# Two-layer transformer block on one core: the heads' way to the output projection, through TensorE's transposes or through DRAM

## What is computed

```python
# B, T, C, H, D = 8, 512, 256, 16, 16
def attend(q, k, v, mask=None):             # heads of 16 columns, scale 1/4
    att = einsum('bhqd,bhkd->bhqk', q, k) * scale
    if mask is not None: att = where(mask, att, -inf)
    return einsum('bhqk,bhkd->bhqd', softmax(att, axis=-1), v)
# layer 0: causal self-attention and cross-attention share the queries' tokens; the two results are added
n = layernorm(x)
y = attend(n @ Wq + bq, n @ Wk + bk, n @ Wv + bv, causal) \
  + attend(n @ Wcq + bcq, ctx @ Wck + bck, ctx @ Wcv + bcv)
x = x + merge_heads(y) @ Wp + bp
x = x + bitlinear(gelu(bitlinear(layernorm(x), w1, b1)), w2, b2)   # int8 per token, ternary weights
# layer 1: cross-attention, then an FFN with one int8 scale for the whole tensor
n = layernorm(x)
x = x + merge_heads(attend(n @ Wq + bq, ctx @ Wk + bk, ctx @ Wv + bv)) @ Wo + bo
x = x + qlinear(gelu(qlinear(layernorm(x), w1, b1)), w2, b2)
```

## Time and profile before

| | |
|---|---|
| median of three runs | 2200.6 us (2190.96 to 2205.16) |
| span of the profiled execution | 2195.8 us |
| TensorE busy | 1773.6 us, 81% |
| VectorE busy | 1367.3 us, 62% |
| ScalarE busy | 1184.4 us, 54% |
| GpSimd busy | 727.3 us, 33% |
| DMA, mean share of 16 engines | 26% on the kernel's own queue |

### The profile page before, as it was taken

One profiled execution on the slowest core, in us unless ns is written; L12 is line 12 of the kernel. 1 busy time (PEld: TensorE's weight loads), 2 busy tenths in 40 slices (PEclk: granted clock), 3 DMA queues, 4 the chain that ended last, 5 costly groups with the idle time before them and its releaser, 6 DMA issues.

```text
span 2195.8 us, 35331 instructions
## 1 busy us (share of the span) xinstructions
PE 1773.6 (81%) x10144; PEld 758.5 (35%) x10144; DVE 1367.3 (62%) x2522; ACT 1184.4 (54%) x2245; POOL 727.3 (33%) x981
## 2 busy tenths in 40 slices
PE   2748488998789879997989788988898788768487
PEld 1214233442344324422443244323442343222124
DVE  2545566667656575667566766676566657354587
ACT  1135247555755566555755484547555754716484
POOL 4214052543244325431553135331543242230012
PEclk8679698999899989998999899998999899869699
DMA  3332331333132312332132213231333121030303
GB/s 105 87 89 59 87 102 30 90 88 104 30 83 74 94 49 73 98 87 56 45 100 77 77 45 97 75 98 31 85 82 95 36 83 35 1 106 1 134 10 124
DMA packets 107134, 160.46 MB, mean 73 GB/s; under 512 B 20673, under 2 KB 83265, under 8 KB 106945
## 3 DMA queue, kind: packets, MB, share of 16 engines
q1 hardware_dynamic: 102048, 156.96, 25.7%
q10 hardware_dynamic: 4896, 1.18, 0.3%
HBM read 105.52 MB, written 51.38 MB: 71 GB/s over the span
## 4 chain that ended last, share of the span: by engine, by line
PE 44%; POOL 14%; DVE 13%; issue 11%; ACT 8%; DMA 6%; SPq 3%; ACTq 0%; DVEq 0%; POOLq 0%
PE acc L1263 10%; PE mx L1228 10%; PE st L1249 8%; DVE nmax L1040 6%; PE misc L1203 4%; PE misc L1175 3%; POOL qk L725 3%; PE misc L1215 3%; POOL parts L727 3%; POOL parts L723 3%; PE misc L1290 2%; POOL parts L729 2%; PE misc L1317 1%; PE misc L1304 1%; DMA hid<-in_L_ffn_w_dram 1%
## 5 line engine op out<-in xcount | busy, mean ns | idle before, releaser
L1040 DVE TENSOR_REDUCE nmax<-mx 128x1 f32<-128x512 f32 (+2 forms) x1376 | 877.8, 673 | 504.6 <-PE mx L1228 313.8
L820 ACT ACTIVATE probs<-st 128x512 f32<-128x512 f32 (+3 forms) x1536 | 771.6, 549 | 592.8 <-PE st L1249 386.2
L1228 PE MATMUL mx<-stack 96*128 96x512 bf16 (+3 forms) x1536 | 570.5, 383 | 205.1 <-DVE nmax L1040 136.5
L1249 PE MATMUL st<-stack 99*128 99x512 bf16 (+3 forms) x1536 | 565.8, 377 | 68.5 <-ACT probs L820 51.0
L1228 PEld LDWEIGHTS mx<-stack 96*128 96x128 bf16 x1536 | 154.2, 101 | 429.6 <-DVE nmax L1040 308.1
L1249 PEld LDWEIGHTS st<-stack 99*128 99x128 bf16 x1536 | 151.5, 100 | 418.6 <-ACT probs L820 249.2
L723 POOL TENSOR_TENSOR parts<-qk,zero 128x512 bf16<-128x512 f32 x96 | 99.7, 1039 | 321.8 <-ACT qk L803 321.8
L735 POOL TENSOR_TENSOR nparts<-nmax,zero 128x16 bf16<-128x16 f32 x96 | 20.5, 214 | 403.8 <-DVE nmax L1040 396.5
L1263 PE MATMUL acc<-probs,v_x 128*32 128x512 f32 x1024 | 153.0, 673 | 0.0
L1263 PE MATMUL acc<-probs,v_f 128*32 128x512 f32 x1024 | 142.5, 630 | 0.4 <-ACT probs L820 0.3
L725 POOL TENSOR_TENSOR qk<-qk,parts 128x512 f32<-128x512 f32 x96 | 111.0, 1156 | 7.5
(11 more groups left out here) (213 smaller groups left out, 2164.1 us busy)
## 6 DMA issues: line engine op xcount, KB each, us to landing
parts_xk<-parts SPq DMA_DIRECT2D x48, 128.0 KB
parts_xq<-parts SPq DMA_DIRECT2D x48, 128.0 KB
stack<-parts_xq SPq DMA_DIRECT2D x32, 192.0 KB, 3.2
stack<-parts_xk SPq DMA_DIRECT2D x32, 192.0 KB, 3.6
parts_sk<-parts SPq DMA_DIRECT2D x48, 128.0 KB
parts_sq<-parts SPq DMA_DIRECT2D x48, 128.0 KB
stack<-parts_sq SPq DMA_DIRECT2D x32, 192.0 KB, 2.8
stack<-parts_sk SPq DMA_DIRECT2D x32, 192.0 KB, 3.3
```

What stands on the lines that cost most here:

```text
L820: act.activation(probs[:, j % P_SLOTS, c, T - w:], st_bank(n, 4 * j + c)[:, 0:w], ACT.Exp, scale=SCALE).then_inc(exp_done, 1)
L1040: dve.tensor_reduce(nmax[:, ring, first:first + NT * (len(cs) - 1) + 1:NT], src, AX.X, ALU.max, negate=True).then_inc(mx_free, 1)
L1228: last = pe.matmul(o, stack[0:ROWS, r, 0, c, P * i:P * i + P], stack[0:ROWS, r, 1, c, 0:w], start=True, stop=not causal)
L1249: last = pe.matmul(o[:, 0:w], stack[0:AUG, r, 1, c, P * j:P * j + P], stack[0:AUG, r, 0, c, T - w:T], start=True, stop=not causal)
```

## The change

The divided heads no longer go through TensorE. They go through DRAM:

- `heads_copy` writes one of two buffers. `heads_send` (SyncE, place 4 of the next slot) stores it, 128 x 512 fp32, 256 KB, to DRAM.
- For each pair of units (g = 1 and g = 3) `pair_fetch` (SyncE, place 7) reads the pair's denominators back densely as 128 x 32 (16 KB), and the 16 rows of each of the eight heads into yT, 128 x 512 (256 KB): the layout that the output projection reads.
- `pair_recip` (VectorE, place 11) takes one reciprocal of 128 x 32; `rec_send` (SyncE, place 12) stores it, 16 KB; `rec_bcast` (SyncE, place 15) reads it back with each head's row repeated on its 16 partitions, 128 x 512.
- `pair_mult` (GpSimd, place 3 of the slot after that) multiplies yT by it. `y_sum` (GpSimd) adds the two attentions in the same layout. In the last turn the last pair of layer 0 takes shorter distances (FAST), and `close` does all of it in a row.
- `heads_out` and `y_T` are gone. There are three yT now, one for each attention.
- Steps move. `ctx_T`, v and the key projections of f (`context1`) move from slots 3 and 4 to slot 0, from place 4 on. `layer1_end` begins in slot 1 at place 4 rather than slot 0 at place 6; layer 0's FFN and the rest of layer 1's start follow it. `layer0_end` moves from slot 8 to slots 9 and 10, with the projections of s behind it in slots 10 and 11. In the last turn `layer0_end` moves from slot 8 to slot 9, and the v of layer 1's last batch stays in AFTER.
- Statistics of the FFN's norm wait for the residual's second read in every batch (before, only in the last). Smaller: the tail's bias row is scaled in place.

```diff
+PLACES = {"heads_send": 4, "pair_fetch": 7, "pair_recip": 11, "rec_send": 12, "rec_bcast": 15}
+FAST = {"heads_send": 3, "pair_fetch": 6, "pair_recip": 8, "rec_send": 8, "rec_bcast": 10, "pair_mult": 13}
...
-            if (j, c) == (1, 1) and prev:
-                out.append(("heads_out", prev))
+            if (j, c) == (0, 3) and pair(back) and not after_fast:
+                out.append(("pair_mult", back))
+            if prev:
+                out += [(name, prev) for name, k in at.items() if k == HU * j + c and (pair(prev) or name == "heads_send")]
...
-    return [("values", u, NT - 1), ("heads_copy", u), ("heads_out", u)]
+    return [("values", u, NT - 1), ("heads_copy", u), ("heads_send", u), ("pair_fetch", u), ("pair_recip", u),
+            ("rec_send", u), ("rec_bcast", u), ("pair_mult", u)]
...
+def project_q(b, p):
+    return [x for m in range(KC) for x in (("project", b, p + "q", m), None, None, None)] + [("settle", b, p)]
...
-    return [("mid_bias", b), ("y_T", b, "A"), None, None, ("residual", b, "A"), None]
+    return [("mid_bias", b), ("y_sum", b), None, None, ("residual", b, "A"), None]
...
-    return [("stats", b, "C"), None, ("ctx_T", b, "C"), None, None, ("norm", b, "C"), None, ("norm_T", b, "C"), None]
+    return [("stats", b, "C"), None, None, None, ("norm", b, "C"), None, ("norm_T", b, "C"), None]
...
+def context1(b):
+    return [("ctx_T", b, "C"), None, ("v", b, "f"), None] + [x for m in range(KC) for x in (("project", b, "fk", m), None, None)]
 
...
-    return layer1_norm(b) + project(b, "f")
+    return layer1_norm(b) + project_q(b, "f")
...
-    return [("y_T", b, "C"), None, ("residual", b, "C"), None, ("stats", b, "E"), None, None, ("norm", b, "E"),
+    return [("residual", b, "C"), None, ("stats", b, "E"), None, None, ("norm", b, "E"),
...
-        start = slots(us[:5], [None] * 6 + layer1_end(b - 2) + layer0_ffn(b - 1) + layer1_start(b - 1), b + more)
+        start = slots(us[:1], [None] * 4 + context1(b - 1), b + more) + \
+            slots(us[1:5], [None] * 6 + layer1_end(b - 2) + layer0_ffn(b - 1) + layer1_start(b - 1), b + more)
...
-            slots(us[8:9], [None] * 6 + layer0_end(b), b) + \
-            slots(us[9:12], layer0_ffn(b) + [("load1", b)] + layer1_norm(b) + project_qk(b, "f"), b)
+            slots(us[8:9], [], b, fast=True) + \
+            slots(us[9:12], layer0_end(b) + layer0_ffn(b) + [("load1", b)] + layer1_norm(b) + \
+                  [("ctx_T", b, "C")] + project_qk(b, "f"), b, after_fast=True)
...
-        slots(us[8:9], [None] * 6 + layer0_end(b), b + more) + \
-        slots(us[9:12], project(b + 1, "s") if more else [], b + more)
+        slots(us[8:9], [], b + more) + \
+        slots(us[9:12], [None] * 6 + layer0_end(b) + (project(b + 1, "s") if more else []), b + more)
...
-        heads = sb("heads", [P, T])
+        heads = sb("heads", [P, 2, T])
...
+        den, rec = sb("den", [P, KPAIR]), sb("rec", [P, KPAIR])
+        spread = sb("spread", [P, T])
...
-        y = {p: sb(f"y_{p}", [P, NT, C]) for p in "xs"}
-        yT = sb("yT", [P, KC, T])
+        yT = {p: sb(f"yT_{p}", [P, KC, T]) for p in "xsf"}
+        y_s = yT["s"][:, :, :].rearrange("p k t -> p (k t)").rearrange("p (t c) -> p t c", c=C)
+        y_x = yT["x"][:, :, :].rearrange("p k t -> p (k t)").rearrange("p (t c) -> p t c", c=C)
...
+            def heads_send(s):
+                r, n, (_, p, g) = s.n.slot(2), s.n, s.unit
+                sp.wait_ge(heads_full, n.at(2))
+                wait_alone(sp)
+                sp.wait_ge(divided, n.round(2).at(1))
+                sp.dma_start(heads_kept[p][g].rearrange("c r t -> (c r) t"), heads[:, r, :]).then_inc(heads_sent[r], 16)
...
+            def pair_fetch(s):
...
+                kept = heads_kept[p][g - 1:g + 1]
+                sp.dma_start(den[:, :], kept[:, :, D, :].rearrange("u c (k t) -> (u c) k t", t=KPAIR)).then_inc(den_in, 16)
+                sp.dma_start(yT[p][:, g // 2, :], kept[:, :, 0:D, :].rearrange("u c d t -> (u c) d t")).then_inc(num_in, 16)
+
+            def rec_send(s):
+                n = s.n.round(2)
+                sp.wait_ge(rec_done, n.at(1))
+                wait_alone(sp)
+                sp.wait_ge(spread_in, n.times(16, 16).at())
+                sp.dma_start(rec_kept.rearrange("(p k) -> p k", p=P), rec[:, :]).then_inc(rec_out, 16)
+
+            def rec_bcast(s):
+                n = s.n.round(2)
+                sp.wait_ge(rec_out, n.times(16, 32).at())
+                wait_alone(sp)
+                sp.wait_ge(divided, n.at(4))
+                sp.dma_start(spread[:, :],
+                             rec_kept.rearrange("(h t) -> h t", t=T).unsqueeze(1).to_broadcast([2 * HU, D, T])).then_inc(spread_in, 16)
...
+            def pair_mult(s):
+                n, (_, p, g) = s.n.round(2), s.unit
+                pool.wait_ge(num_in, n.times(16, 32).at())
+                pool.wait_ge(spread_in, n.times(16, 32).at())
+                y_ = yT[p][:, g // 2, :]
+                pool.tensor_tensor(y_, y_, spread[:, :], ALU.mult).then_inc(divided, 1)
+
+            def y_sum(s):
+                last_pair = Count(AT[s.key[1], "s", NU - 1], PER_TURN, s.i).round(2)
+                pool.wait_ge(divided, last_pair.at(5))
+                pool.tensor_tensor(yT["s"][:, :, :], yT["s"][:, :, :], yT["x"][:, :, :], ALU.add).then_inc(y_summed, 1)
 
...
-
-                if s.n.base or s.i is not None:
-                    act.wait_ge(rsum_done, s.n.at())
-                act.copy(heads[:, :], acc[:, :]).then_inc(heads_full, 1)
-
-            def y_T(s):
-                for m in range(KC):
-                    copy_misc(s, m, yT[:, m, :])
+                act.wait_ge(heads_sent[s.n.slot(2)], s.n.round(2).times(16, 16).at())
+                act.copy(heads[:, s.n.slot(2), :], acc[:, :]).then_inc(heads_full, 1)
...
-                if k == "F" and last_batch(s):
+                if k == "F":
...
-            def heads_out(s):
...
-                dve.reciprocal(rsum[:, s.n.slot(4), :, :], o[:, :, :, D]).then_inc(rsum_done, 1)
...
-                dve.tensor_tensor(y[p][:, :, HU * D * g:HU * D * (g + 1)].rearrange("p t (c d) -> p t c d", d=D),
-                                  o[:, :, :, 0:D], rsum[:, s.n.slot(4), :, :].unsqueeze(3).to_broadcast([P, NT, HU, D]),
-                                  ALU.mult).then_inc(misc_free[slot], 1)
+            def pair_recip(s):
+                n = s.n.round(2)
+                dve.wait_ge(den_in, n.times(16, 16).at())
+                dve.wait_ge(rec_out, n.times(16, 16).at())
+                dve.reciprocal(rec[:, :], den[:, :]).then_inc(rec_done, 1)
...
-            def heads_out(s):
-                pe.wait_ge(heads_full, s.n.at(2))
-                turn_tiles(s, 0, [heads[:, P * t:P * t + P] for t in range(NT)], ident)
-
-            def y_T(s):
+            def residual(s):
                 k = s.args[0]
...
-                    reads = [misc_read(s, 0, ("heads_out", (s.key[1], "f", NU - 1)))]
-                y_ = y["s"] if k == "A" else y["f"]
-                for m in range(KC):
-                    turn_tiles(s, m, [y_[:, t, P * m:P * m + P] for t in range(NT)], ident, reads=reads)
-
-            def residual(s):
-                k = s.args[0]
-                reads = [misc_read(s, m, ("y_T", s.key[1], k)) for m in range(KC)]
+                    last_pair = Count(AT[s.key[1], "f", NU - 1], PER_TURN, s.i).round(2)
+                    pe.wait_ge(divided, last_pair.at(5))
                 for h in range(2):
-                    wait_misc(pe, s, h, reads)
+                    wait_misc(pe, s, h, ())
                     for t in range(2):
                         first = P * (2 * h + t)
                         for m in range(KC):
-                            last = pe.matmul(misc[misc_slot(s, h)][:, C * t:C * t + C], yT[:, m, first:first + P],
```

80 lines of the change are left out of this document (46 added, 34 removed).

## The result

The changed kernel took 2477.25 us (median of four runs, 2471.88 to 2484.92), the kernel before beside it 2202.88 us: a ratio of 1.1259, 95% interval 1.1217 to 1.1301. I had forecast 2240, between 2150 and 2290. The sign was right, the size was not: +274 where I had +39.

A forecast was written before the change was run, and what follows sets the result against it. TensorE was taken to set the pace in a turn's middle and last stages. Per turn 8.4 + 4.0 + 2.8 + 2.0 - 14.0 = +3.2; with turn 0 and the bare ends +38.8, so 2240 us, range 2150 to 2290.

The forecast's parts named there:

- Work taken from it comes back in full: Middle and last stages of a turn: TensorE, busy 44.5 of 50.7 and 67.8 of 73.2 us, sets the pace.
- the FFN's shift: FFN one slot later: about four causal reductions beside it fall away on VectorE, 2.8 us gained per turn.
- The wait in slot 1: TensorE's residual of layer 1 waits 8.4 us per turn for GpSimd's product, bounds 1.5 to 9.5.
- The wait in slot 6: VectorE's reciprocal waits for denominators fetched behind a key projection's store, costing 4.0 us per turn.
- Slot 5: that cover takes it: nothing: Product waits behind query stores, but TensorE's existing 3.1 us wait covers it: nothing; 1 to 3 us if that failed.
- Slot 8 and slot 0: Slots 8 and 9: TensorE stops gaining, 2.0 us per turn; no wait for the context load in slot 0 counted.
- The clock: Half clock after a long wait: one loss of 2.8 us counted per turn, bounds 0 to 5.6.
- The bare ends: Exposed pair chains after the last turn, +8.8 us, and at the very end, +9.6; together +18.4, bounds 14 to 22.
- The turning point: The kernel gets slower once the waits in slots 1 and 6 exceed about 7 us together.
- Worse than forecast: Late product in slot 1 also holds GpSimd's statistics, second clock loss: +10 us per turn, 2287 us; chance 0.15.
- covered: Rival: the waits in slots 1 and 6 are hidden, -10 us per turn, 2145 us; chance 0.20.
- one wait only: Rival: slot 6's wait is hidden with its clock loss, -3.6 us per turn, 2192 us; chance 0.18.

The follow-up runs named there:

- ctx_early: The changed kernel with layer 1's context load issued in slot 5 of the turn before: 2423.81 us, ratio 1.1027 to the kernel before.
- sp_order: The changed kernel with only SyncE's list reordered, projection stores behind the spread and settles just ahead of the first stack needing them: 2313.98 us, ratio 1.0524.
- best2: The changed kernel with SyncE's list reordered, context load earlier, last turn's end dealt over slots, residual, reciprocal and product later: 2254.1 us, ratio 1.0263.

## Why the prediction was wrong, step by step

**"Work taken from it comes back in full."** Wrong, and the first step that failed. I read TensorE's 67.8 busy of 73.2 us as a pace. A score or maximum matmul stands in the profile with 0.38 us in the mean where the next can start after 0.22, so a TensorE that is held up a little at every maximum can still show as busy. What its busy time was worth, the two runs show. In the five loop turns, from slot 0 to slot 0, the 240 transposes are worth 31.8 us by their spacing (60 times 0.53). Without them TensorE was busy for 27.1 us less and idle for 7.0 more, and the turns took 20.1 less; with them twice it was busy for 28.3 more and idle for 9.5 less, and the turns took 18.8 more. And the last stage, where I had the full return, gave least: its slots 8 to 11 hold 2.1 us of transposes, and took 72.1 us before, 71.6 without them and 73.5 with them twice. The Trainium skill has a warning for this (Perfetto Trace Analysis, "Identifying the Most-Contended Engine"): matmul busy share is no good measure of how near a kernel is to its limit, since the instructions are pipelined, and the busy share of the weight loads is one of two figures to use instead. The trace fits that: in the last stage the weight loads were busy for 25.2 of the 73.2 us. Per turn, the 7.7 us for the heads' transposes and their VectorE work measured 3.7 (five turns: 1155.5 to 1137.1). The 2.8 for the FFN's shift can't be told apart, but all moves together gave 0.9 per turn (1155.5 to 1150.8), so it was not there in full. The y transposes' 3.5 were not tried alone.

**The wait in slot 1.** Right in place and mechanism, 10.2 against 8.4, but that the sizes are so near is in part luck. I had TensorE at the residual 15.5 us after the heads copy and the product done after 23.9; it was 24.6 and 34.7, both behind the late context load, which I did not have. With that load early (ctx_early) it was 25.2 and 28.9, and the wait 3.7. The product (1.26 us, I had 1.15) stood behind the spread, the spread behind the second parts_fk, as the order rows said. The spread took 5.5 us from its issue to the product (1123.16 to 1128.68) where I had 3.4; at the bare end 4.0.

**The wait in slot 6.** Right, 5.2 against 4.0; VectorE's reciprocal stood there for 6.1 us, where I had 3 to 5.

**"Slot 5: that cover takes it: nothing."** Wrong, and the same mechanism as in slot 1, which I had seen there and priced at 1 to 3 us here if the cover failed. The stack's 3.1 us covered 3.1 of 7.6. sp_order shows the cause: with the spread ahead of the stores the wait falls to 1.5 and the stack's own.

**Slot 8 and slot 0: not in the sum.** For slot 8 I counted only what TensorE loses in gain, and never followed the heads' sending through SyncE, behind the settle and the stacks. The cx_C load I did not look at, although the change moves its reader from slot 3 to slot 0; a step that moves earlier has to be asked for all its inputs. The waits: 4.8 and 4.9 us in the third turn, the second 6.3 in the mean of the five. Taking the load's lateness away gave 7.4 per turn (ctx_early), though by way of slot 1.

**The clock.** I counted one loss of 2.8 us per turn; there were five waits. TensorE was busy 208.2 us in the turn after, and 201.4 in the same turn of best2, which has the same matmuls: 6.9 us, at a mean clock of 0.87 rather than 0.92; in the mean of the five turns it is 9.4. Over five waits that is 1.4 to 1.9 us each, where I had 2.8, so the count was too low and the size too high. The lower clock itself came behind each of the five, 0.50 to 0.69 in the 5.7 us after it. best2 is not free of it either, with a wait of 3.6 us in slot 5 and 0.50 behind it.

**The bare ends.** At the very end 13.1 us were forecast from the end of the last heads copy to the residual; it took 12.7 (2285.05 to 2297.72), with 2.0 for the heads, where I had 3.2, and 4.0 for the spread, where I had 3.4:

```profile
2284.46 0.59 ACT L906 COPY heads<-acc 128x512 f32<-128x512 f32 x1 [1.19 <-PE acc L1328]
2285.13 0.33 SPq L660 DMA_DIRECT2D heads_f<-heads  x1
2287.36 0.60 SPq L678 DMA_DIRECT2D den<-heads_f  x1
...
2289.54 0.35 DVE L1122 RECIPROCAL rec<-den 128x32 f32<-128x32 f32 x1 [18.91 <-DMA den<-heads_f]
2290.00 0.32 SPq L686 DMA_DIRECT2D rec_kept<-rec  x1
2292.41 0.60 SPq L693 DMA_DIRECT2D spread<-rec_kept  x1
2296.41 1.26 POOL L822 TENSOR_TENSOR yT_f<-yT_f,spread 128x512 f32<-128x512 f32 x1 [17.89 <-DMA spread<-rec_kept]
2297.72 1.35 PEld L1345 LDWEIGHTS misc<-W_Co,yT_f 128*128 128x128 f32 x4 [14.24 <-POOL yT_f L822]
```

The other end was +8.8 in the prediction and is about +23 (from the copy of batch 6's last unit to that of f0 of batch 7: 60.9 before, 83.6 after). I had the four transfers, but not that the sending stands behind four projections' stores: the heads were copied at 2169.1 and sent at 2182.89.

**The turning point.** I wrote that the kernel gets slower once the two waits exceed 7 us together. The waits came to 29.6, and the gain they had to beat was nearer 5 (3.7 for the transposes, 0.9 for the moves, the y transposes not tried) than 14.

**The rivals.** "Worse than forecast" had the mechanism that came, a late product that holds GpSimd's statistics, and was put at +10 us per turn and 2287 in all; the order on the queue did it, or the like, in five places of a turn. The two rivals below the forecast, covered and one wait only, rested on a gain of 14 us per turn that is not there.

What was right: the sign, its reason (a chain behind other engines' waits on SyncE), and the two places named. What made the size wrong: three more waits, and a gain counted from busy time. Put into the sum for a turn, with the figures above: waits of 29.6 for 12.4 add 17.2, the clock 4 to 7, a gain of 5 for 14 another 9; with the forecast's 3.2 that is an estimated 34 to 36, measured 34.5. The waits are the larger half of the miss. Two small slips in the working change nothing of this: the turn before took 233.4 us by the earlier trace rows, not 232, and the 12 KB row was issued by ScalarE, not SyncE.

How the excess divides, in medians, from the changed kernel down, each as it came in this order: stores out of the chain 139 us, settles 25, the context's load 27 (53 if taken alone first, so the shares depend on the order), the last turn's end 15, residual and reciprocal later 18. What is left, 2254 against 2210 for the moves alone, is 44: in the traces of the two (spans 2244.5 and 2209.3) 11.8 lies in the five turns, 12.7 in the last, 11.9 at the very end, 5.9 ahead of batch 1, 3.0 in the last three units, and turn 1 is 10.0 shorter. What exactly the last turn's 12.7 are was not tried; the two kernels also differ there in the slot of layer 0's end. So the order on the queue is shown for most of the excess, and the last 44 us stay open.

## What to carry to other kernels

When a change puts a chain of transfers on a queue that is shared and in order, list every place where the chain occurs, not the one or two where it looks tight, and at each ask what stands ahead and what that waits for. A store whose data are not ready yet belongs behind everything in the queue that is ready. A busy share of 93% is no proof that an engine sets the pace: look whether its short waits for one partner recur, and do the suspected work twice or not at all before counting it as gain. And when a wait is taken away, look in the trace where the time came back: it need not be there.

## What the runs showed of the hardware

- Taking away five waits for one load, 32.0 us together in turns 3 to 7 (4.9 to 9.6 each), shortened the five turns by 37.2 us (ctx_early), but waits of about the same size came up in the same slot, and the gain lay in the next one. What a wait takes does not say what its removal gives.
- The same 256 KB spread took 4.0 us from issue to the product's start with the queues otherwise empty (2292.41 to 2296.41), and 3.6 to 6.6 (median 5.0) over all the products of the changed kernel that waited for it. By the Trainium skill (DMA: Bandwidth & Descriptors, "Anatomy of one DMA") 256 KB should take an estimated 2.6 us, by a formula for transfers issued from GpSimd; the trace does not agree for the spread, issued from SyncE, whose bytes come from 16 KB read sixteen times. By the Trainium skill (the same page, "Rules for kernel authors") a transfer is spread over no more engines than its outermost dimension has elements, and the spread's is eight heads; no run here shows that. A heads store of 256 KB let its fetch start 2.2 us after its issue at the bare end (2285.13 to 2287.36), and 4.1 us after it in slot 8, behind six stack DMAs (1287.74 to 1291.79).
- VectorE's reciprocal of 128 x 32 took 0.35 us for two units, where the two of 128 x 16 took 0.25 each: the dense form saves 0.15 us per pair, in a chain of 12.7 at the bare end.
